# The causal-mask multiplies of an attention stage issued on VectorE in place of GpSimd

## The reference, cut to what matters

```python
scores = jnp.einsum('bhqd,bhkd->bhqk', Qh, Kh) / jnp.sqrt(jnp.float32(dk))   # dk = 64
scores = jnp.where(causal, scores, jnp.float32(-1e+30))
attn = jax.nn.softmax(scores, axis=-1)
out = jnp.einsum('bhqk,bhkd->bhqd', attn, Vh)
...
return jnp.concatenate(head_outs, axis=-1) @ W_O
```

## Time and profile before

| what | value |
|---|---|
| median of 3 runs | 6606.65 us |
| the profiled execution's own time | 6597.3 us |
| its span on the slowest core (core 5) | 6595.8 us |
| spans of the 8 cores | 6538.3 to 6595.8 us |
| PE (TensorE matmul) busy | 4922.2 us, 75% |
| DVE (VectorE) busy | 1526.6 us, 23% |
| POOL (GpSimd) busy | 1304.8 us, 20% |
| ACT (ScalarE) busy | 1164.3 us, 18% |
| mean granted TensorE clock | 0.851 of full speed |

### The profile page before, as it was taken

The page is one execution under the profiler, slowest core; times in us unless marked ns, Lnnn a source line. Parts: engine busy times, 40 slices in busy tenths (PEclk is TensorE's granted clock), DMA queues, the critical chain, the costliest instruction groups (busy, mean ns, idle before and its releaser), DMA issues.

```text
span 6595.8 us, 62003 instructions; the slowest of 8 cores (6538.3 to 6595.8 us)
## 1 busy us (share of the span) xinstructions
PE 4922.2 (75%) x20400; PEld 1843.0 (28%) x20400; DVE 1526.6 (23%) x2035; ACT 1164.3 (18%) x1301; POOL 1304.8 (20%) x1568
## 2 busy tenths in 40 slices
PE   0688887454555666577659999978899499988884
PEld 0233332010111111111124444433334144433331
DVE  0112221012002000200034444410004544440004
ACT  0000001323442553466600000000000000000000
POOL 0000002643541443233300000012210000002220
PEclk9999997566667677777779999999999599999996
DMA  9422334021013111211035555568875255549883
GB/s 148 70 50 59 60 64 96 20 78 47 29 36 96 39 39 64 84 39 39 33 77 96 96 96 96 96 147 169 189 147 96 71 96 96 96 82 192 177 186 104
DMA packets 360624, 592.63 MB, mean 90 GB/s; under 512 B 85504, under 2 KB 208576, under 8 KB 357056
## 3 DMA queue, kind: packets, MB, share of 16 engines
q0 software_dynamic: 155968, 260.75, 26.5%
q1 hardware_dynamic: 204352, 327.92, 15.9%
HBM read 767.26 MB, written 88.28 MB: 130 GB/s over the span
## 4 chain that ended last, share of the span: by engine, by line
PE 48%; DMA 15%; POOL 13%; DVE 8%; ACT 6%; issue 6%; another core or an unknown queue 3%; DVEq 0%; POOLq 0%; ACTq 0%; SPq 0%
PE ps L744 13%; PE ps L754 13%; POOL ar L552 13%; DMA ar<-wd 8%; PE ps L871 7%; DMA vspill<-ar 5%; ACT ar L540 4%; PE ps L348 4%; PE ps L571 2%; PE ps L517 2%; DMA ar<-wospill 2%; PE ps L441 2%; PE ps L679 1%; PE ps L982 1%
## 5 line engine op out<-in xcount | busy, mean ns | idle before, releaser
L744 PE MATMUL ps<-ar 128*128 128x512 bf16 x4096 | 1222.0, 380 | 64.7 <-DMA ar<-wg 33.1
L754 PE MATMUL ps<-ar 128*128 128x512 bf16 x4096 | 1221.7, 380 | 2.9 <-DMA ar<-wu 2.9
L571 PE MATMUL ps<-ar 128*65 128x512 bf16 x1920 | 756.6, 484 | 476.3 <-POOL ar L552 476.3
L871 PE MATMUL ps<-ar 128*128 128x512 bf16 x4096 | 944.2, 386 | 197.9 <-DMA ar<-wd 125.1
L552 POOL TENSOR_TENSOR ar<-ar 128x512 bf16<-128x512 bf16 x768 | 868.8, 1150 | 978.7 <-ACT ar L540 922.8
L540 ACT ACTIVATE ar<-ps 128x1024 bf16<-128x1024 f32 x960 | 906.4, 1081 | 356.9 <-PE ps L525 284.8
L871 PEld LDWEIGHTS ps<-ar 128*128 128x128 bf16 x4096 | 392.7, 99 | 749.4 <-issue 335.6
L744 PEld LDWEIGHTS ps<-ar 128*128 128x128 bf16 x4096 | 401.3, 98 | 551.9 <-issue 71.3
L754 PEld LDWEIGHTS ps<-ar 128*128 128x128 bf16 x4096 | 401.4, 98 | 489.4 <-issue 8.4
L517 PE MATMUL ps<-ar 64*128 64x512 bf16 x960 | 433.5, 472 | 132.0 <-DVE ar L1086 75.5
L774 ACT ACTIVATE ar<-ps 128x1024 bf16<-128x1024 f32 x128 | 131.2, 1025 | 2190.5 <-PE ps L744 1561.5
(11 more groups left out here) (103 smaller groups left out, 2634.4 us busy)
## 6 DMA issues: line engine op xcount, KB each, us to landing
ar<-hspill SPq DMA_DIRECT2D x512, 256.0 KB, 4.7
ar<-wg POOLq DMA_DIRECT2D x128, 512.0 KB, 5.7
ar<-wu POOLq DMA_DIRECT2D x128, 512.0 KB, 8.3
ar<-wd POOLq DMA_DIRECT2D x512, 128.0 KB, 4.9
ar<-wospill SPq DMA_DIRECT2D x72, 512.0 KB, 3.7
hspill<-ar SPq DMA_DIRECT2D x128, 256.0 KB, 6.0
ar<-xT POOLq DMA_DIRECT2D x8, 2048.0 KB, 20.7
ar<-xTo POOLq DMA_DIRECT2D x8, 2048.0 KB, 15.8
```

The lines of the kernel that those rows point to most:

```text
L571: st=st, ste=ste: e.matmul(bank(6 + hd, rows=65), vstg[:, 130 * c + 65 * hd: 130 * c + 65 * hd + 65], eap[:, hd * 512:(hd + 1) * 512], sta ...
L744: lambda e, bb=bb, th=th, kc=kc, s=s, wgs=wgs: e.matmul(bank(bb + th), wgs[:, kc * 128:(kc + 1) * 128], x1[:, kc * 2048 + s * 512: kc * 20 ...
L754: lambda e, bb=bb, th=th, kc=kc, s=s, wus=wus: e.matmul(bank(bb + 2 + th), wus[:, kc * 128:(kc + 1) * 128], x1[:, kc * 2048 + s * 512: kc ...
L871: lambda e, bi=bi, ft=ft, th=th, ic=ic, wst=wst, hst=hst: e.matmul(bank(bi), wst[:, ft * 128:(ft + 1) * 128], hst[:, th * 512:(th + 1) * 512],
```

## The change

The two mask multiplies of a masked chunk are issued on VectorE and raise `sv`; before, they were issued on GpSimd and raised `sg`. Their operands, their count and what waits for them are the same.

```diff
@@ -548,14 +548,14 @@
                         midx = j - (ext - 2)
                         for hd in range(2):
                             evmk = kb.emit(
-                                "gpsimd",
+                                "vector",
                                 lambda e, eap=eap, midx=midx, sub=sub, hd=hd: e.tensor_tensor(
                                     eap[:, hd * 512:(hd + 1) * 512],
                                     eap[:, hd * 512:(hd + 1) * 512],
                                     A(msk_o + midx * 2048 + sub * 512, 512),
                                     ALU.mult),
                                 waits=eB.rd_waits() + list(eB.w_ev.items()) + B["msk"].rd_waits(),
-                                inc="sg")
+                                inc="sv")
                             eB.add_write(evmk)
                             B["msk"].note_read(evmk)
```

## The result

The changed kernel is faster by more than forecast: its time is 0.9119 of the kernel before (95% interval 0.91 to 0.9139). Of the 6606.65 us shown ahead that is 6025 us, a gain of 582 us (569 to 595) where 532 were forecast. Executions in which one die or both ran at a lower granted clock (in the changed kernel's first profile 0.81 for 4215 us of a span of 6506) are left out of the ratio, on both sides. Its numbers are compared with those of before pass by pass, not as a whole.

What follows compares the result with a forecast made beforehand. The prediction took POOL's 48 blocks of 16 mask multiplies to bound the passes. Gains of 400 us (36 passes, tiles 1 to 3) and 132 us (12 passes, tile 0) sum to 532: 6606.65 - 532 = 6075 us, range 6040 to 6200.

Steps and rivals of the forecast that it cites:

- 0.14 + 0.59 + 0.11: From a block's end to copy L595: a delay, the last two value matmuls at the upper clock, a delay, in us.
- rivals of a dearer operation (0.69, 1.225): Mask multiplies on VectorE cost 0.692 us (6290 us in all, chance 0.04) or 1.225 us (6700 us, chance 0.03).
- slower: In the mask block, VectorE costs more than POOL did: 1.33 us a mask with the gap, 6700 us; chance 0.03.
- I charge the gap to all: Each VectorE mask multiply takes 0.425 us plus a 0.105 us gap: 1.06 us a chunk, 8.4 us a block.
- ScalarE ... stays ahead: In masked chunks ScalarE takes 0.94 us, faster than VectorE's 1.06, so it does not set the pace.
- The range: For the whole kernel's time: the forecast's own 6045 to 6105 us, extended to 6200 for passes losing the clock.
- the clock's best case, 29 us: If the clock stays up after the tail, spreads and first scores gain at most 29 us; counted as 0.
- 6105: Upper end, in us, of the forecast's own range, with tile 0 at the lower clock.
- The rival of the lower clock: TensorE stays at the lower clock in masked chunks: gain 362 us, 6245 us; chance 0.06.
- The limit named by the Trainium skill: Dense matmuls on three or more cores of a die held at 1.95 GHz: 75 us of gain lost; chance 0.01.

Runs made afterwards that it cites:

- e10_chain: The changed kernel, with each mask multiply also waiting for whatever VectorE issued just ahead; ratio 0.9175 to the kernel before, or 6062 us.
- e8_twice_free: The changed kernel with every mask multiply issued twice, each waiting only for the earlier one on its own half; 6198.37 us in one execution, no ratio.

## Why the prediction missed

**The path before** was read rightly: the masks' block of 16 on POOL held each pass, and moving it gave back 12.2 of the 13.4 us a pass that the masks had cost. The copies come 0.84 us after the block, as the forecast's 0.14 + 0.59 + 0.11 had it at the upper clock, and L642 and L649 cost nothing ahead of the masks.

**The price of the operation**, 0.425 us, was right. So the rivals of a dearer operation (0.69, 1.225) fell, and "slower" with them.

**The failed step** is the sentence "Every second mask multiply waits for the one before it, and the others for ScalarE, so I charge the gap to all." The gap of 0.105 read from the earlier trace rows is that of an operation that waits for the one just ahead on VectorE. The others don't wait for it, and can start 0.34 us after it, under its last 0.08. VectorE needs 0.53 + 0.34 = 0.87 us for a pair, not 1.06. That is under ScalarE's 0.92 to 0.94, so the forecast's "ScalarE ... stays ahead" fell with it: a masked chunk goes at ScalarE's pace, and the block is 7.4 us, not 8.4. In tile 0, where TensorE starts each pass at the lower clock, it is 7.9. Over 48 passes (12 x 0.54 + 36 x 1.02) that is 43 of the 52 us by which 584 exceeds 532. The other 9 are the last two value matmuls. In nearly all passes they ran at the upper clock, which shortens the way from the block to the copy by 0.44 us, and the forecast had taken some 0.25 of that in tiles 1 to 3 and 0.15 in tile 0. e10_chain puts the gap back for all, gets 8.36 us for the block and gives 39 us back; e8_twice_free takes the wait away from all and gets steps of 0.34.

A row of the trace before showed it. The two copies at a pass's end have no wait between them, and the second starts 0.61 us after the first (L595 at 1113.78 in the earlier trace rows), which lasts 0.69:

```profile
1114.39 0.68 DVE L599 CAST ar<-ps 65x512 bf16<-65x512 f32 x1
```

**The range** failed with it: its lower end took only the clock's best case, 29 us, and no lower bound for the gap, though two kinds of neighbour stood in the trace. Two small slips in the working moved nothing: 6105 should be 6100 (6075 and 12 x 2.1), and 1.2025 us is the block's 19.24 divided by 16, where from start to start it is (19.24 - 1.15) / 15 = 1.206.

**The clock** did what was expected. The four tiles have 0.72, 0.80, 0.83 and 0.87 where windows of the same tiles before gave 0.50, 0.67, 0.70 and 0.74. The full clock was forecast for the masked chunks of tiles 1 to 3 and for the second half of those of tile 0. By the clock's records the blocks of tiles 1 to 3 stand at 1.00, and those of tile 0 at 0.53 in their first half and 0.91 in their second. Windows inside a block of tile 0, the first and second half, and of tiles 1 and 3:

```profile
1161.00:1165.00 4.00, 3.99 (x12) 0.86 (x12) 3.53 (x9) 4.00 (x5) 0.00 (x0) 0.50 0.00 0
1165.00:1169.00 4.00, 3.75 (x15) 1.11 (x14) 2.99 (x8) 2.58 (x3) 0.00 (x0) 0.86 0.20 42
1487.00:1494.00 7.00, 6.55 (x30) 1.79 (x28) 6.17 (x16) 6.00 (x7) 0.00 (x0) 1.00 0.19 56
2403.00:2410.00 7.00, 5.95 (x26) 1.54 (x24) 6.11 (x15) 5.84 (x7) 0.00 (x0) 1.00 0.31 98
```

The rival of the lower clock fell. From 2412 to 2420, in the tail and the next pass's first rounds, the clock was down again at 0.50, so nothing was gained there, as counted. The limit named by the Trainium skill, "TensorE: Matmul & The Clock Gate", Part 1, did not show in this profile: it would be 0.81 (1.95 of 2.4 GHz), and the windows grant 1.00 in masked chunks and 0.95 in the feed-forward. But the 0.81 named at the head of the section on the result is that very level. The prediction's "The trace disagrees with it here" is thus true of the traces compared here, and not of the chip; what brings the limit on stays open.

## What to carry to other kernels

When work moves to an engine, price it as a chain: duration, then the step to the next instruction, once for a neighbour that it waits for and once for one that it doesn't. Find a pair of each kind in the trace before charging one of them to all. And compare the result with the next engine's pace: here 0.1 us a mask (1.06 or 0.87 for a pair, against ScalarE's 0.92) decided which engine set the time of a chunk.

## What the runs showed of the hardware

On VectorE, bf16 multiplies of 128x512 in SBUF, 0.42 us each by the trace, follow each other every 0.34 us if the second doesn't wait for the first, also when it carries a wait that is already met (32 in 11.03 us, e8_twice_free). They follow every 0.53 us if it does (16 in 8.36 us, e10_chain). The wait for the operation just ahead costs 0.19 us, more than half of the free step.
